# A new order for the attention's batches, with weight products in the prefix and gate products later

## What is computed

```python
# block 1, attention over 256 tokens, 8 heads of 16
Q, K, V = x @ Wq + bq, x @ Wk + bk, x @ Wv + bv
qq, kq = Q @ Wc2q + bc2q, K @ Wc2q + bc2q          # 8 features a head
fid = qq @ kq.T / max(|qq| |kq|, EPS_COS)
aw = 0.5 * fid * (1 + 0.1 * sin(pi * fid)) + 0.5 * Q @ K.T / 4
attn = softmax(aw) @ V @ Wo + bo
x1 = layernorm(x + attn); qm = (x1 @ W1 + b1) @ Wm + bm
ff = ((tanh(qm) * cos(qm * pi / 4)) @ Wqo + bqo) @ W2 + b2
out = layernorm(x1 + ff)
# block 2, one of 8 experts a token
expert = argmax(x @ gate_w); out = prob * (gelu(x @ w1[e] + b1[e]) @ w2[e] + b2[e])
```

## Time and profile before

| what | us |
|---|---|
| median of 3 runs | 550.81 |
| profiled execution, time | 552.67 |
| profiled execution, span | 550.9 |
| prefix, to the first sine | 0 to 72.5 |
| batch 0 | 72.5 to 95.6 |
| batches 2 to 13 | 111.2 to 288.3 |
| attention ends | 318.0 |
| post stage | 318 to 432 |
| FFN | 434 to 551 |

### The profile page before, as it was taken

How to read it: one execution, slowest core, us unless ns; L and a number is a source line. 1 busy time by engine, 2 the same in 40 slices (tenths; PEclk the granted TensorE clock), 3 DMA queues, 4 the chain that set the end, 5 groups by cost and what they waited for, 6 DMA issues and landing times.

```text
span 550.9 us, 9018 instructions
## 1 busy us (share of the span) xinstructions
PE 393.9 (72%) x2668; PEld 282.0 (51%) x2668; DVE 368.5 (67%) x887; ACT 339.8 (62%) x715; POOL 267.0 (48%) x399
## 2 busy tenths in 40 slices
PE   0978688888888888888888788664000399999960
PEld 0754366555555555555555433663000288888850
DVE  4886557788888888888888524549983016666670
ACT  0244346788898888888888735864210277778740
POOL 8364016444444444444440012374877207787874
PEclk9979859899999999999999989967555589999995
DMA  9560203355445555555552899900111215666500
GB/s 210 29 153 20 60 23 88 89 136 137 117 117 138 134 133 121 128 126 131 130 122 67 106 140 132 237 5 11 35 40 54 80 39 155 199 192 201 175 14 0
DMA packets 81245, 58.19 MB, mean 106 GB/s; under 512 B 17619, under 2 KB 72919, under 8 KB 81196
## 3 DMA queue, kind: packets, MB, share of 16 engines
q1 hardware_dynamic: 75142, 53.12, 44.3%
q0 software_dynamic: 2496, 4.29, 2.3%
q10 hardware_dynamic: 3558, 0.20, 0.5%
HBM read 35.38 MB, written 23.11 MB: 106 GB/s over the span
## 4 chain that ended last, share of the span: by engine, by line
PE 35%; issue 21%; DVE 15%; ACT 14%; SPq 9%; POOL 2%; DMA 2%; ACTq 1%; POOLq 0%; DVEq 0%
PE ps L1559 8%; DVE mxs L1719 7%; PE ps L1570 7%; ACT big L920 5%; SPq L518 4%; ACT big L910 4%; SPq L557 3%; DVE big L1798 3%; PE ps L1374 3%; PE ps L1367 3%; PE ps L1387 3%; PE ps L1352 2%; PE ps L1229 2%; ACT proj L861 2%; DVE gb L1633 1%
## 5 line engine op out<-in xcount | busy, mean ns | idle before, releaser
L1719 DVE TENSOR_REDUCE mxs<-ps 128x4 f32<-128x1024 f32 x64 | 76.6, 1218 | 21.5 <-PE ps L1229 20.4
L1768 DVE SCALAR_TENSOR_TENSOR big<-big,ps 128x1024 f32<-128x1024 f32 x64 | 74.6, 1216 | 2.5 <-ACT big L910 2.5
L910 ACT ACTIVATE big<-ps 128x1024 f32<-128x1024 f32 x64 | 61.9, 1012 | 7.4 <-PE ps L1352 7.2
L694 POOL CAST mtok<-mxs 128x8 bf16<-128x8 f32 x32 | 6.0, 189 | 115.1 <-DVE mxs L1719 115.1
L1798 DVE TENSOR_TENSOR big<-big,ps 128x1024 f32<-128x1024 f32 x32 | 38.9, 1216 | 25.5 <-PE ps L1374 25.5
L811 POOL DMA_INDIRECT out_dram<-arena,fidx x46 | 46.7, 1016 | 17.9 <-issue 16.4
L1352 PE MATMUL ps<-proj 128*128 128x256 f16 x256 | 40.7, 286 | 19.4 <-DVE mxs L1719 14.1
L1229 PE MATMUL ps<-arena 96*128 96x256 bf16 x256 | 39.1, 276 | 18.5 <-ACT big L920 13.9
L2104 DVE TENSOR_SCALAR arena<-ps,x_all 128x128 f32<-128x128 f32 x46 | 14.0, 347 | 56.8 <-PE ps L1579 48.8
L1559 PE MATMUL ps<-arena,big 128*128 128x256 f32 x184 | 47.2, 403 | 1.1 <-ACT arena L1125 1.1
L1119 ACT ACTIVATE x_all<-x_all 128x128 f32<-128x128 f32 x46 | 20.1, 486 | 44.2 <-DMA x_all<-sorted_rows 42.0
(11 more groups left out here) (341 smaller groups left out, 963.7 us busy)
## 6 DMA issues: line engine op xcount, KB each, us to landing
big<-in_L_ffn_w_dram SPq DMA_DIRECT2D x46, 256.0 KB
qk_parts<-proj SPq DMA_DIRECT2D x16, 384.0 KB, 3.2
arena<-qk_parts SPq DMA_DIRECT2D x32, 192.0 KB, 3.5
sorted_rows<-zrow SPq DMA_DIRECT2D x16, 266.0 KB, 3.7
arena<-qk_parts SPq DMA_DIRECT2D x32, 128.0 KB, 4.0
proj<-u_parts SPq DMA_DIRECT2D x48, 64.0 KB
x_all<-sorted_rows SPq DMA_DIRECT2D x23, 133.0 KB
sorted_rows<-zrow SPq DMA_DIRECT2D x2, 1263.5 KB, 26.8
```

The source lines that it names most:

```text
L910: nc.scalar.activation(W[par][:, n, :], src, ACT.Sin, scale=PI * (1 - 1e-6)).then_inc(sin_ready, 1)
L1719: nc.vector.tensor_reduce(mxs[:, b1 % 2, :, 2 * n:2 * n + 2], src, AX_X, ALU.max, negate=True).then_inc(unit_free, 1)
L1768: nc.vector.scalar_tensor_tensor(W[par][:, n, :], W[par][:, n, :], 10.0, f, ALU.add, ALU.mult).then_inc(unit_free, 1)
```

## The change

- The maxima are computed two batches ahead: eight max units come before batch 0, and batch b makes those of b + 2. q and k go three batches ahead (QK0); those of batch 2 are made in the prefix.
- The order of the units in a batch is cos 0, 1, 3, 2, log 1, 0, 3, max 3, 2, log 2, max 0, 1, and all engines follow it. Both turned maxima of b + 1 are handled in batch b, pv and heads_out of b - 1 come before the exponentials of b, and all four exponentials of b are in batch b.
- The weight products run inside the prefix (after the groups 3, 4, 6 and after the last), in banks 4 and 5.
- The gate products of x move to the post stage, in two halves; y is therefore stored elsewhere than xnT (y_of).
- ln_stats(0 to 2) come before the first loads of weights are waited for; the reciprocal std0 moves to the start of the post stage.

Cut to its core (8 columns of indent removed):

```diff
+def wbank(k):
+    return ps[:, 4 + k % 2, :]
...
+def y_of(g):
+    if g == NG - 1:
+        return bigf[:, DEPTH * 2 * EF:DEPTH * 2 * EF + GT * P]
+    return projf[:, NT * ROW + g * GT * P:NT * ROW + (g + 1) * GT * P]
...
+QK0 = 3
+turns = [("u", 0), ("u", 1), ("m0", 0), ("m1", 0)]
+turns_before = []
 for b in range(NB):
-    turns += [("m1", b)] + [(k, b + d) for k, d in (("qk", 2), ("u", 2), ("m0", 1)) if b + d < NB]
+    turns_before.append(len(turns))
+    turns += [(k, b + d) for k, d in (("qk", QK0), ("u", 2), ("m0", 1), ("m1", 1)) if b + d < NB]
 turn_no = {k: i for i, k in enumerate(turns)}
-units = [("max", 0, n) for n in range(HP)]
+sin_order = (0, 1, 3, 2)
+units = [("max", b, n) for b in range(2) for n in range(HP)]
 for b in range(NB):
-    units += [("cos", b, n) for n in range(HP)]
-    for k, d, n in (("log", 0, 0), ("max", 1, 0), ("log", 0, 1), ("max", 1, 1), ("log", 0, 2), ("log", 0, 3), ("max", 1, 2), ("max", 1, 3)):
+    units += [("cos", b, n) for n in sin_order]
+    for k, d, n in (("log", 0, 1), ("log", 0, 0), ("log", 0, 3), ("max", 2, 3), ("max", 2, 2), ("log", 0, 2), ("max", 2, 0), ("max", 2, 1)):
         if b + d < NB:
             units.append((k, b + d, n))
...
-        eng.wait_ge(p_ready, HP * b + n + 1)
+        eng.wait_ge(p_ready, HP * b + sin_order.index(n) + 1)
...
-    put_max(0, 0)
-    get_max(0, 0)
+    put_qk(2)
+    get_qk(2)
+    for r in range(2):
+        put_max(0, r)
+        get_max(0, r)
...
     def body(b, par, first, last, slow):
-        put_max(b, 1)
-        if 2 <= b + 1 < NB:
-            get_u(b + 1)
-        get_max(b, 1)
-        zeros(ZA)
+        if b + QK0 < NB:
+            put_qk(b + QK0)
         if b + 2 < NB:
-            put_qk(b + 2)
             put_u(b + 2)
         if not last:
             put_max(b + 1, 0)
+            put_max(b + 1, 1)
+            get_max(b + 1, 0)
+        if b + QK0 < NB:
+            get_qk(b + QK0)
+        if not last:
+            get_max(b + 1, 1)
         if b + 2 < NB:
-            get_qk(b + 2)
-        if not last:
-            get_max(b + 1, 0)
+            get_u(b + 2)
+        zeros(ZA)
...
     def body(b, par, first, last, slow):
-        split_max(b, 1)
+        if not last:
+            split_max(b + 1, 0)
         if b + 2 < NB:
             split_u(b + 2)
-            split_qk(b + 2)
         if not last:
-            split_max(b + 1, 0)
+            split_max(b + 1, 1)
+        if b + QK0 < NB:
+            split_qk(b + QK0)
         xb = x_all[:, b * TPB:(b + 1) * TPB, :]
         nc.gpsimd.tensor_tensor(xb, xb, mv_all[:, 0, b * TPB:(b + 1) * TPB].unsqueeze(2).to_broadcast([P, TPB, C]), ALU.subtract)
         if first:
             root_out()
     split_max(0, 0)
+    split_max(0, 1)
     batches(pool, body, False)
...
         take_v(g)
         squares(g)
-        if g == 3:
+        if g == 2:
             roots(0)
-    take_u(0)
-    take_u(1)
+            take_qk(2, ps[:, 4, :])
+        if g >= NG - 2:
+            take_u(g - NG + 2)
+        if g in (3, 4, 6, 7):
+            weights((3, 4, 6, 7).index(g) + 1)
     roots(1)
-    act.wait_ge(step["xg"], 1)
-    nc.scalar.copy(usq[0], ps[:, 5, :]).then_inc(step["xg"], 1)
     nc.scalar.activation(hT[:, 0:1], halfpi[:, 0:1], ACT.Sin)
     def body(b, par, first, last, slow):
         def sin(n):
             if slow:
-                act.wait_ge(g_f, b * HP + n + 1)
+                act.wait_ge(g_f, b * HP + sin_order.index(n) + 1)
                 src = g_cos
...
-        if first and slow:
+        if first:
             take_max(0, 0)
+            take_max(0, 1)
         sin(0)
-        if first and not slow:
-            take_max(0, 0)
         sin(1)
-        take_max(b, 1)
+        sin(3)
+        if b + QK0 < NB:
+            take_qk(b + QK0, tbank)
         sin(2)
-        sin(3)
+        if not first:
+            heads_out(b - 1)
+        exp(b, par, 0)
+        if b + 2 < NB:
+            take_u(b + 2)
+        exp(b, par, 1)
+        exp(b, par, 3)
+        if not last:
+            take_max(b + 1, 0)
+        exp(b, par, 2)
         if first:
-            weights(1)
-        if b + 2 < NB:
-            take_qk(b + 2, tbank)
-        if not first:
-            exp(b - 1, 1 - par, HP - 1)
-        for n in range(HP - 1):
-            exp(b, par, n)
-            if first:
-                weights(n + 2)
-            if first and n == HP - 2:
-                nc.scalar.activation(hT[:, 0:1], halfpi[:, 0:1], ACT.Sin)
-            if n == 0 and b + 2 < NB:
-                take_u(b + 2)
-            if n == 1 and not first:
-                heads_out(b - 1)
-            if n == 1 and not last:
-                take_max(b + 1, 0)
+            nc.scalar.activation(hT[:, 0:1], halfpi[:, 0:1], ACT.Sin)
+        if not last:
+            take_max(b + 1, 1)
         if last:
-            exp(b, par, HP - 1)
             heads_out(b)
...
+    def take_gates(h):
+        act.wait_ge(step["xg"], 4 * h + 1)
+        nc.scalar.copy(gx_s, ps[0:64, 3, :]).then_inc(step["xg"], 1)
...
     turn_qe(5)
+    take_gates(0)
     square_t(3)
...
+    take_gates(1)
     square_t(7)
...
     def max_unit(b1, n):
-        if n == 0:
-            pe.wait_ge(qk_in[b1 % 3], 96 * (b1 // 3 + 1))
+        pe.wait_ge(qk_in[b1 % 3], 96 * (b1 // 3 + 1))
...
+        pe.wait_ge(consts_ready, 27)
+        pe.wait_ge(qk_out, 3)
...
     for g in range(NG):
         make_uv(g)
         if g + 2 < NG:
             turn_x(g + 2)
-        if g == GH:
-            pe.wait_ge(qk_out, 2)
-            pe.wait_ge(consts_ready, 28)
-        if GH <= g < NG - 1:
-            gate_x(2 * (g - GH))
-            gate_x(2 * (g - GH) + 1)
-    turn_u(0)
+        if g == 1:
+            pe.wait_ge(qk_out, 1)
+            make_qk(2, ps[:, 4, :])
+        if g == 3:
+            weights_1()
+        if g == 4:
+            weights_2()
+        if g == 6:
+            turn_u(0)
+            weights_3()
     turn_u(1)
-    gate_x(NG - 2)
-    gate_x(NG - 1).then_inc(step["xg"], 1)
+    weights_4()
...
-    pe.wait_ge(step["xg"], 4)
+    pe.wait_ge(w_act, 4)
...
             max_unit(0, 3)
-        if first and slow:
             turn_max(0, 0)
+            max_unit(1, 0)
+            turn_max(0, 1)
+            for n in range(1, HP):
+                max_unit(1, n)
+        if b == 2:
+            pe.wait_ge(set_cp, 3)
+            pe.wait_ge(w_dve, 2)
...
         cos_unit(0)
-        if first and not slow:
-            turn_max(0, 0)
         cos_unit(1)
+        if b + QK0 < NB:
+            bank_free("qk", b + QK0)
+            make_qk(b + QK0, tbank)
+        cos_unit(3)
+        if not first:
+            pv(b - 1, 1 - par, 0)
         cos_unit(2)
-        turn_max(b, 1)
-        cos_unit(3)
-        if first:
-            weights_1()
-        if b + 2 < NB:
-            bank_free("qk", b + 2)
-            make_qk(b + 2, tbank)
+        if not first:
+            pv(b - 1, 1 - par, 1)
+        logit_unit(1)
         logit_unit(0)
-        if not last:
-            max_unit(b + 1, 0)
-        if first:
-            weights_2()
-        logit_unit(1)
+        logit_unit(3)
         if b + 2 < NB:
             turn_u(b + 2)
-        if b == 1:
-            pe.wait_ge(w_act, 4)
-        if b == 2:
-            pe.wait_ge(set_cp, 3)
-            pe.wait_ge(w_dve, 2)
-        if not first:
-            pv(b - 1, 1 - par, 0)
-        if not last:
-            max_unit(b + 1, 1)
-        if first:
-            weights_3()
-        logit_unit(2)
-        if not first:
-            pv(b - 1, 1 - par, 1)
-        logit_unit(3)
+            max_unit(b + 2, 3)
+            max_unit(b + 2, 2)
         if not last:
             turn_max(b + 1, 0)
+        logit_unit(2)
+        if b + 2 < NB:
+            max_unit(b + 2, 0)
+        if not last:
+            turn_max(b + 1, 1)
         if not first:
             heads_back(b - 1)
-        if not last:
-            max_unit(b + 1, 2)
-        if first:
-            weights_4()
-        if not last:
-            max_unit(b + 1, 3)
+        if b + 2 < NB:
+            max_unit(b + 2, 1)
         if last:
             pv(b, par, 0)
...
+    def gate_x(g):
+        h = g // GH
+        return nc.tensor.matmul(ps[0:64, 3, :], gw_at[:, g % GH, :], xnT[:, g * GT * P:(g + 1) * GT * P],
...
+    def turn_gates(h):
+        pe.wait_ge(step["xg"], 4 * h + 2)
+        for i in range(GT):
+            mm = nc.tensor.transpose(ps[:, 3, i * 64:(i + 1) * 64], gx_s[:, i * P:(i + 1) * P], ident[0:64, 0:64])
...
             if g % GH == 0:
                 turn_qe(g)
                 turn_qe(g + 1)
+            if g == GH:
+                gate_x(2)
+                gate_x(3).then_inc(step["xg"], 1)
             second_sum(g)
+            if g == GH - 1:
+                pe.wait_ge(consts_ready, 31)
+                pe.wait_ge(step["q8"], 2)
+                gate_x(0)
+                gate_x(1)
+            if g == GH + 1:
+                turn_gates(0)
```

(74 more changed lines are left out.)

175 lines of the change are left out of this document (75 added, 100 removed).

## The result

The changed kernel takes **518.9 us** (median of 4 runs, 518.01 to 521.55) against 550.4 before: a ratio of 0.9436, 95% interval 0.9397 to 0.9474. The forecast was 511, range 505 to 528: faster as forecast, inside the range, 7.9 us above the number. The profiled execution has a span of 518.0 and a time of 519.75.

A forecast was written before the change was run, and what follows sets the result against it. A ring of waits, with no engine full, was taken to bound the batches. Profiled 552.67 minus 40.6 up to the attention's end plus 0.7 in the post stage gave 512.8; the median, 1.86 lower, gave 511 us, range 505 to 528.

The forecast's parts named there:

- a ring of waits: Steady batches before the change: late PSUM slots and PE's written order set the 14.76 us batch, no engine filling it.
- 12.5: Steady batch after the change: ACT's summed work in us with nothing idle, 2.26 less than before.
- The two waits of the earlier trace: Steady batches before: DVE stands 1.6 us a batch for a logit unit, ACT 1.6 for the head sums.
- 11.2: Steady batch: PE's summed work in us, below ACT's 12.5 and DVE's 12.2.
- the flag at 63.0: Prefix: flag written at 63.0 instead of 64.82, as the pair of gate groups no longer stands between.
- rival A: Prefix: the weights' product steps stall the uv groups, the whole 8.3 us stay, time 519; chance 0.07.
- 14.8: Batch 0: a steady 12.5 plus 2.3 for the uncovered reciprocal of 2.54 on DVE.
- 0.1, or 3.2 ... I take the high clock: Post stage: take_gates(1) waits for 8 products, delay 0.1 at PE's high clock, 3.2 at the low; high one taken.
- the 540: Batches: time if two DMA hops 1.8 us longer each bring the stack 2.2 late in each of 13.
- rival B: Batches: stack or turned maxima land late; hops 1.2 us longer each cost 13 more, 524; chance 0.08.
- C: Batches: TensorE's clock falls; at the 1.2 GHz level 105 us more, 616; chance 0.02.
- D: Batches: another slot wait replaces the ring, 1 us or more a batch, 525 and up; chance 0.08.

The follow-up runs named there:

- e5: Changed kernel with one more 128x512 copy on ACT in every batch, between exp 1 and exp 3; 526.78 us (one run).
- e6: Changed kernel with one more 128x512 sum on DVE in every batch, ahead of the heads' division; 524.37 us (one run).
- e2: Changed kernel with weights_3 behind the last uv group and weights_4 behind the two flag products on PE, ACT copies following; 515.10 us.
- e4: Changed kernel with the four weight products back in batch 0, through hbank, new unit order kept; 522.41 us.
- e7: Changed kernel with e1's and e2's edits, plus weights_4 in the turned tiles' bank and batch 0's second turned maximum one unit later; 512.31 us.
- e1: Changed kernel with ACT's copy take_gates(1) moved behind square_t(7) in the post stage; 516.54 us.

## Why the prediction was right, and where it was off

**The mechanism.** It held: a ring of waits bound the batch, the change as a whole (maxima two batches ahead, new order of units) breaks it, and then ACT's sum is the period (e5, e6). 12.5 was forecast from the intervals of the earlier trace rows, 12.39 measured. Twelve batches gave 28.0 us of the 32.9. The two waits of the earlier trace rows went, ACT shows no gap, DVE 0.2 to 0.4 (e6), PE's clock is 1.00. PE's sum was forecast 11.2 and is 142.93/12 = 11.9; it stayed under ACT's, so nothing hung on it.

**Prefix, branch and batch 0: +5.1 us over the forecast, the largest miss.** It is 3.3 up to the first weight, 1.6 in batch 0 and 0.2 behind it. The step that failed is "the flag at 63.0 ... since the pair of gate groups no longer stands between". The pair went, and weights_3, 2.8 us of PE, took its place ahead of the last uv group. I had summed the weights' products as if they filled PE's gaps beside the uv groups; the third one stood on the path. e2 took it out and the flag came 2.6 earlier. From flag to first weight the forecast held (12.6 on paper, 12.8 measured). This is rival A in part, 3.3 us of its 8.3: with no products in the prefix the first weight is 3.2 earlier (e4). But the one step is not all of it: with it moved the first weight came only 1.0 earlier, and another 1.3 came when the fourth product's bank and the order of the turned maxima were changed too (e7).

Batch 0 was forecast 14.8 from the earlier trace rows's reciprocal alone and took 16.3 from first weight to the next: besides the reciprocal ACT stood 2.2 for the logit behind it and DVE 1.3 for a maximum unit. Batch 1 took 13.9 and not 12.5. In batch 1 PE stood 1.35 for the turned maxima from DRAM, whose gets had gone out 4.5 us after their first put (90.20, 94.68; usual 1.5). The paper sum had steady handovers in batches that start with empty slots and late transfers. That the stretch from batch 1 to the end of the attention came out right, 188.3 us against 188.1, is in part luck: batch 1 (13.5 from first sine to first sine) and the late batch were 1.0 and 0.5 over the forecast, the ten other batches up to batch 12 0.1 each and the last three together 0.2 under it.

**Post stage: +1.8 us.** The step is "0.1, or 3.2 ... I take the high clock". Eight matmuls took 4.67 us, between the 3.7 and the 6.8 of the two bounds, and the last root on POOL came 2.2 late. The bounds held the value, the choice of the lower one was wrong: a stage with a mean clock of 0.57 in the earlier trace rows gives no reason to take the high level. Better still, the copy had another place to stand (e1), where its length doesn't count.

**Handovers by DMA.** Median landings were 3.0 for put_qk and 4.0 for a get (3.2 and 4.0) though the rate rose from 128 to 149 GB/s, so the 2 us of an HBM access at high load (the Trainium skill, DMA: Bandwidth & Descriptors, "Latency and other measured facts") do not show in the medians, and the 540 that they would have given did not come. The 192 KB get rose from 3.5 to 3.7. The one or two late batches in an execution fit a scatter of single landings, not a shift: rival B at 0.5 to 4.9 us an execution instead of 13.

**C and D** did not occur in the steady batches: clock 1.00, and no slot took over. The low clock came in one batch of e1 alone.

**The remainder** is 1.0 us of difference between the profiled execution and the median (0.85 now, 1.86 before), which no profile could tell.
